# Setup of an attention and expert kernel: VectorE writes the rows of ones first, in 32-bit words, and each weight load has a semaphore of its own

## The reference

```python
qkv = x @ Wqkv + bqkv                       # 16 heads of 16
scores = stack([(q * shift(k, d)).sum(-1) for d in OFFSETS]) * scale + pos_bias.T
alpha = softmax(where(invalid, -inf, scores))
out = sum(alpha[..., i] * shift(v, d) for i, d in enumerate(OFFSETS))
x = layernorm(x + (out * sigmoid(x @ Wgate + bgate)) @ Wout + bout)
logits = relu(x @ rw1 + rb1) @ rw2 + rb2    # router, top 2 of 8 experts
h = relu(disp @ ew1 + eb1);  eo = h @ ew2 + eb2
x = layernorm(x + sum_k prob_k * eo[expert_k, slot_k])
```

## Time and profile before

| | us |
|---|---|
| median of 3 runs | 2030.01 |
| lowest and highest of them | 2027.12, 2035.88 |
| the profiled execution, own time | 2021.59 |
| its span, first to last instruction | 2019.9 |

### The profile page before, as it was taken

How to read it: one execution, slowest core, us unless ns; L and a number is a source line. 1 busy time by engine, 2 the same in 40 slices (tenths; PEclk the granted TensorE clock), 3 DMA queues, 4 the chain that set the end, 5 groups by cost and what they waited for, 6 DMA issues and landing times. The chain is left out here.

```text
span 2019.9 us, 72320 instructions
## 1 busy us (share of the span) xinstructions
PE 1514.6 (75%) x31232; PEld 1005.1 (50%) x31232; DVE 988.9 (49%) x2117; ACT 905.3 (45%) x1544; POOL 705.7 (35%) x654
## 2 busy tenths in 40 slices
PE   0555787877787787878777887878765499999980
PEld 0234455555454555445554555545553266676660
DVE  4213445554545554555545544564644355555525
ACT  1231443635354453535444453544433365655626
POOL 4221313525333342525333342534323113323335
PEclk9765777868787777868787777868876699999995
DMA  2464624345352524335342524335220333443428
GB/s 77 74 171 156 134 56 98 98 77 125 80 114 79 108 73 93 97 70 115 85 98 75 105 70 88 91 78 110 58 57 14 108 105 85 95 114 85 74 28 337
DMA packets 220103, 194.55 MB, mean 96 GB/s; under 512 B 66847, under 2 KB 207151, under 8 KB 219648
## 3 DMA queue, kind: packets, MB, share of 16 engines
q1 hardware_dynamic: 204464, 175.11, 35.0%
q0 software_dynamic: 15360, 15.10, 4.7%
HBM read 98.07 MB, written 86.18 MB: 91 GB/s over the span
## 5 line engine op out<-in xcount | busy, mean ns | idle before, releaser
L394 POOL TENSOR_TENSOR p<-p 128x512 f16<-128x512 f32 x96 | 129.3, 1347 | 434.3 <-ACT p L794 434.2
L808 ACT COPY featT<-gp 128x1024 f16<-128x1024 f16 x96 | 93.3, 1031 | 329.3 <-PE gp L539 329.3
L394 DVE TENSOR_TENSOR p<-p 128x512 f16<-128x512 f32 x96 | 94.3, 982 | 288.0 <-ACT p L794 287.5
L546 PE MATMUL gp<-featT,wr 128*128 128x512 f16 x768 | 198.8, 416 | 24.2 <-DVE mT L957 15.4
L1105 POOL DMA_INDIRECT disp<-y,sidx x128 | 175.7, 1372 | 53.5 <-issue 37.9
L1359 POOL DMA_INDIRECT xln<-y,place x64 | 104.9, 1640 | 216.4 <-DVE y L1501 175.9
L1397 PE MATMUL up<-rowsT,w 128*128 128x512 f16 x768 | 170.1, 381 | 10.3 <-DVE w L1474 5.3
L1411 PE MATMUL dn<-w,h 128*128 128x256 f16 x1536 | 170.1, 273 | 0.0
L621 PE MATMUL o<-v_near,p 128*32 128x66 f16 x2048 | 134.6, 204 | 40.6 <-issue 29.1
L793 ACT ACTIVATE p<-st 128x512 f16<-128x512 f32 x192 | 116.6, 607 | 102.7 <-PE st L590 98.7
L1411 PEld LDWEIGHTS dn<-w,h 128*128 128x128 f16 x1536 | 149.7, 98 | 17.3
(11 more groups left out here) (176 smaller groups left out, 3138.1 us busy)
## 6 DMA issues: line engine op xcount, KB each, us to landing
qk_dram<-qk SPq DMA_DIRECT2D x64, 256.0 KB, 2.5
v_near<-vs SPq DMA_DIRECT2D x224, 66.0 KB
qs<-qk_dram SPq DMA_DIRECT2D x96, 128.0 KB, 4.6
ks<-qk_dram SPq DMA_DIRECT2D x96, 128.0 KB, 7.4
o_dram<-o_far SPq DMA_DIRECT2D x64, 136.0 KB, 5.7
o_back<-o_dram SPq DMA_DIRECT2D x16, 544.0 KB, 3.9
v_dram<-vs SPq DMA_DIRECT2D x16, 528.0 KB
v_far<-v_dram SPq DMA_DIRECT2D x64, 132.0 KB
```

Source lines behind the costliest of these rows:

```text
L394: engine.tensor_tensor(p16[:, b, 1, :], p32[:, b, :], p16[:, b, 0, :], ALU.subtract).then_inc(is_split, 1)
L546: last = nc.tensor.matmul(dst, lhs(a, c), rhs(b, c), start=(k == 0), stop=(k == len(todo) - 1))
L808: gp_done(nc.scalar.copy(featT[:, i, :, :].rearrange("f c t -> f (c t)"), bank[:, :].bitcast(F16)), n, stage, PART_OF_T[stage], i)
```

## The change

The fills of `ks` stand at the head of VectorE's program in `setup` and no longer at its end. Each writes the same bytes as 32 partitions x 2048 words of float32, whose bit pattern is two float16 ones. The first six loads (five weights and pos_bias) each get a semaphore of their own, `here[0]` to `here[5]`; the other nine still share `loaded`. ScalarE waits before each high part for the weight that it reads, and for `loaded` only ahead of the scaling of `bqk`. VectorE waits for pos_bias alone. GpSimd's program and the order of SyncE's DMAs are as before.

```diff
+TWO_ONES = struct.unpack("<f", struct.pack("<I", 0x3C003C00))[0]
...
+        here = [sem(f"setup_in{i}") for i in range(6)]
...
             @block.sync
             def _(sp):
-                for dst, src in loads:
-                    sp.dma_start(dst, src, allow_slow_non_contiguous=True).then_inc(loaded, 16)
+                for k, (dst, src) in enumerate(loads):
+                    sp.dma_start(dst, src, allow_slow_non_contiguous=True).then_inc(here[k] if k < 6 else loaded, 16)
...
             @block.scalar
             def _(act):
-                act.wait_ge(loaded, 16 * len(loads))
-                for src, h, _ in splits:
+                for (src, h, _), k in zip(splits, (0, 0, 1, 2, 3, 4)):
+                    act.wait_ge(here[k], 16)
                     nc.scalar.activation(h, src, ACT.Copy, scale=WS).then_inc(hi, 1)
+                act.wait_ge(loaded, 16 * (len(loads) - 6))
                 nc.scalar.mul(a["bqk"][:, 0:2], a["bqk"][:, 0:2], HD ** -0.5)
...
             @block.vector
             def _(dve):
+                for i in range(2):
+                    for e in range(2):
+                        nc.vector.memset(a["ks"][i][STACK * e + 32:STACK * (e + 1), :, :].bitcast(FP32), TWO_ONES)
                 for v in (vec_n[0], vec_f[0]):
                     nc.vector.memset(v, NEG16)
...
-                dve.wait_ge(loaded, 16 * len(loads))
+                dve.wait_ge(here[5], 16)
                 nc.vector.tensor_copy(pb_16[0], pb_t).then_inc(vec_base, 1)
...
-                for i in range(2):
-                    for e in range(2):
-                        nc.vector.memset(a["ks"][i][STACK * e + 32:STACK * (e + 1), :, :], 1.0)
```

More of the change, by code:

```diff
@@ L3 @@
 from contextlib import ExitStack
+import struct
 FP32 = mybir.dt.float32
@@ L1153, in setup @@
         hi, lo = sem("setup_hi"), sem("setup_lo")
+        here = [sem(f"setup_in{i}") for i in range(6)]
         base, vec_base, vec_done, biased = sem("setup_base"), sem("vec_base"), sem("vec_done"), sem("setup_biased")
         loads = [(qkv_s, tiles(g["Wqkv"])), (gate_s, tiles(g["Wgate"])), (out_s, tiles(g["Wout"])), (r1_s, tiles(g["rw1"])),
-                 (r2_s, tiles(g["rw2"])), (pb_t, g["pos_bias"].rearrange("o h -> h o")),
+                 (r2_s, tiles(g["rw2"])),
+                 (pb_t, g["pos_bias"].rearrange("o h -> h o")),
                  (a["bqk"][:, :], g["bqkv"][0:2 * D].rearrange("(u p) -> p u", p=P)),
```

## The result

The changed kernel takes 2010.79 us in the median of 13 runs, the kernel before 2027.12 in the median of 13 runs beside it. The ratio is 0.9915 with a 95% interval of 0.9896 to 0.9935, so it is faster by 17.2 us (13.2 to 21.1), which is 1 - 0.9915 of the time before; the two medians lie 16.3 us apart. Its profiled execution took 2000.77 us, with a span of 1999.0; that is 20.8 us under the one before (2021.59).

The account below looks back on a forecast made before the run. It took `setup`, which nothing covers, as the bound: 17.46 us from the moved fills and 2.27 from the cast make 19.7 us less, from the median of 2030.01 to 2010.3 us, range 2003 to 2017.

Parts of the forecast that it names:

- Nothing covers `setup`: Before the attention block: TensorE idles for the first 47.28 us, so each microsecond cut from `setup` shortens the whole by one.
- The fills: VectorE's `ks` fills at the head of `setup`: 2.21 us for each 2048 words, 8.84 us for four.
- case 4: Rival on the `ks` fills: words cost as much as their halves; 17.7 us less, 2012.3 us; chance 0.07.
- case 5: Rival in `setup`: fills of VectorE and GpSimd exclude each other; 10.5 us less, 2019.5 us; chance 0.03.
- The cast held by the fill of `v_far`: VectorE's pos_bias cast, ready at 10.6, waits for GpSimd's fill and ends at 16.82 instead of 19.09.
- What follows the cast: VectorE's copies and low parts shift by 2.27 us, ending at 27.28, when the last bias vector lands too.
- GpSimd ends at 23.25 as before: GpSimd's program in `setup` keeps its old times and ends at 23.25 us, before the low parts at 27.28.
- second case: Rival in `setup`: cast free, GpSimd's selects held by VectorE's low parts; 21.1 us less, 2008.9 us; chance 0.2.
- `halfneg` at 23.15: Sign in GpSimd's timeline in `setup`: `halfneg` starts at 23.15 us, or at 25.8 if its selects are held.
- Held until 21.1: Rival's step: GpSimd's selects wait for VectorE's long low part until 21.1; GpSimd's remaining 4.77 us end at 25.9.
- The split of the gain: Of 19.7 us less `setup`, 17.46 come from fills leaving the tail and 2.27 from the earlier cast.
- case 6: Rival behind `setup`: the clock falls from 0.79; 0.78 costs 19.4 us, 0.77 gives 2049.6 us; chance 0.02.

Follow-up runs that it names:

- e8: Changed kernel with the cast on ScalarE, GpSimd's selects ahead of its two long fills, these in 32-bit words: 1953.91 us, ratio to before 0.9886, `xin` at 21.91.
- e12: The changed kernel run again beside the kernel before: 1962.91 against 1979.01 us, ratio 0.9913, `xin` issued at 28.96 us.
- e1: Kernel before with the `ks` fills as 32-bit words, still at the end of `setup`: `xin` issued at 37.91 us instead of 47.28.
- e4: Changed kernel with the cast of pos_bias on ScalarE instead of VectorE: `xin` issued at 26.41 us.
- e5: Changed kernel with GpSimd's `v_far` fill as 4224 words, the same bytes: `xin` issued at 25.44 us.
- e9: Changed kernel with GpSimd's `v_far` fill cut into four fills of 2112 elements: `xin` issued at 26.89 us.
- e7: Changed kernel with a one-column VectorE fill behind each low part: `xin` issued at 27.63 us instead of 28.69.
- e10: Kernel before with only its 16-bit `ks` fills moved to VectorE's head: `xin` issued at 29.68 us instead of 47.28.
- e3: Changed kernel with one semaphore for all 15 loads again: `xin` issued at 29.08 us.
- e6: Changed kernel with GpSimd's fills of `v_near` and `v_far` moved behind its selects and `halfneg`: `xin` issued at 34.08 us or 34.09 (one value per execution).
- e11: Repetition of the changed kernel with GpSimd's two long fills behind its selects and `halfneg`: cast 12.63 us long, `xin` at 34.08 or 34.09 us.
- e2: Changed kernel with its `ks` fills in 16-bit elements, still first: `xin` issued at 29.65 us.

## Why the prediction was right, point by point

- *Nothing covers `setup`.* Shown: in all thirteen other profiled executions `xin` starts 0.27 to 0.37 us behind the last engine, whether that ends early (`xin` at 21.91) or late (37.91). The ones timed several times (e8, e12, the changed kernel) gain about what their `setup` does: 25.1, 16.1 and 16.3 us by the medians, 22.6, 17.2 and 17.2 by the ratios, for 25.4, 18.3 and 18.6 (each 0.9 less by the estimate at e1).
- *The fills.* 2.21 us forecast, 2.23 measured; case 4 (a word costs as much as its halves) and case 5 (the fills exclude each other) are out, the latter by the `v_far` fill at 9.65 in every run that left it there.
- *The cast held by the fill of `v_far`*, the term that was inferred from a row with another kind of GpSimd instruction: 16.96 measured, 16.82 forecast. e4, e5 and e9 show it to be the fill, by moving the cast to another engine, halving the fill and cutting it in four.
- *What follows the cast.* The low parts ended at 27.42 (27.28 forecast), and the last bias vector landed at about 23.55 + 0.63 + 3.2 = 27.4.
- *"GpSimd ends at 23.25 as before"* is the step that failed. The prediction moved the low parts forward to 21.94 and left GpSimd's program at its old times, where the last select runs from 22.15 to 22.36. By its own numbers the two meet. It priced such a meeting only in its second case and put nothing here, without a reason. The last select was caught, and for all six low parts. GpSimd ended last, at 28.39, where 27.28 was to set the end, so the missing term is 1.1 us, and the sum 18.6 instead of 19.7. The length of the hold is what made it cost anything: a select held for one low part, which is the rule of the second case, leaves GpSimd done at 24.10 (e7), far ahead of 27.3. The sign that the prediction named, `halfneg` at 23.15, came out at 28.29, and e7 gives most of that microsecond back.
- *"Held until 21.1"* in the second case took the select to wait for the long low part. In e4, which is that case made real, it waited for the run of all, until 21.67. `xin` came at 26.41, where 26.2 was forecast.
- *The split of the gain.* The prediction gave 17.46 us to the moved fills and 2.27 to the separate signal of pos_bias. The runs give 17.6 to the move (e10), and about 0.6 to the words and 0.1 to 0.4 to the signals on top of it. The 2.27 counted from a cast that ended at 19.09, behind the last landing at 18.9. With one signal and the landing at 17.4 (e3) it ended at 18.26, so the signal gained 1.3 us at the cast, and most of that was lost at the select.
- *The clock* stayed at 0.79 behind `setup`; case 6 is out.

The predicted median, 2010.3, and the measured one, 2010.79, agree to 0.5 us by luck. The forecast gain was 19.7 us and the gain between the medians 16.3; it was taken from 2030.01, the median of the first three runs of before, and that of the thirteen is 2.9 us lower. The two errors cancel.

## What to carry to other kernels

Where no work of the main part can start before setup is over, every microsecond of it counts in full, and moving work from the tail into a wait at the head is worth more than making it faster. Here the width alone gave 8.5 us at the tail and the move alone 17.6; behind the move, width and signals together gave about one. Before a VectorE cast is let go earlier, look which GpSimd instruction runs at the new place; before a run of two-input VectorE instructions is moved, look whether GpSimd has reads of SBUF behind it. A short VectorE instruction without SBUF inputs between them can be cheaper than none, as in the one execution of e7.

## What the runs showed of the hardware that I had not expected

- An unbroken run of VectorE instructions with two SBUF inputs held one GpSimd select through all of them that were left: 5.34 us in the changed kernel, 5.65 in e5 and e12, 3.18 and 3.51 in e4 and e9, each ending 0.06 to 0.17 us behind the last of the run. With a fill of one column between them it was let in behind the first (1.05 us, e7). The 80 copies, of one input, held no select. That it is the second input was not varied alone. The Trainium skill (SBUF — State Buffer, "Who interferes with whom") says that VectorE with two SBUF inputs contends with a GpSimd instruction that reads SBUF and not with one that only writes. These runs agree: the subtraction ran in 0.19 us beside the fill in e4. The length of the hold is in these runs that of the whole run of instructions.
- A GpSimd fill, which reads nothing, holds a VectorE cast of 16x40 elements, and this can last over more than one fill: 12.44 and 12.63 us with two fills back to back (e6, e11), 0.83 us through the last short ones (e3).
- The 80 single-column copies went at 0.06 us each in every run, beside selects (before) and beside `v_far` in 16-bit form (e4, 4.93 us for all from 11.30).
- The row of a large VectorE fill starts late: 1.76 us long at distances of 2.23, and 3.47 at 4.36. As VectorE's first instruction the row starts at 1.30 with 2048 words and at 1.72 with 4096 halves (e2), where a small fill starts at 0.88 (e1). Distances tell its cost.
- GpSimd's fill went from 7.07 us (16.72 - 9.65) to 3.56 (e5) with the same bytes in 32-bit words.
